# Reordering the fronts of five stages over more PSUM banks, and making the expert-choice logits inside the rotary attention

## The reference

```python
x = _layernorm(x + _L0_attn_ref(x, ...))              # latent attention, causal: 16 heads of 64, keys and values from 64 latent columns
x = _layernorm(x + _L0_xattn_ref(x, ctx_1024, ...))   # cross attention, q and k normed, rotary q: 16 heads of 16
x = _layernorm(x + _L0_ffn_ref(x, ...))               # expert choice
x = _layernorm(x + _L1_attn_ref(x, ...))              # t5 attention with a bias by relative position: 16 heads of 64
x = _layernorm(x + _L1_xattn_ref(x, ctx_1024, ...))   # cross attention, 16 heads of 16
x = _layernorm(x + _L1_ffn_ref(x, ...))               # rmsnorm, self attention, rmsnorm, mixture of experts
```

```python
logits = jnp.einsum('bsd,ed->bse', x, gate_w)
affinity = jax.nn.softmax(logits, axis=-1)
affinity = jnp.transpose(affinity, (0, 2, 1))
gating, idx = jax.lax.top_k(affinity, k)      # each expert takes its k best tokens
```

## Time and profile before

| | us |
|---|---|
| median of 3 runs | 2243.45 |
| the three runs | 2232.38, 2243.45, 2246.34 |
| the profiled execution | 2236.97 |
| its span in the trace | 2235.3 |

### The profile page before, as it was taken

How to read it: one execution, slowest core, us unless ns; L and a number is a source line. 1 busy time by engine, 2 the same in 40 slices (tenths; PEclk the granted TensorE clock), 3 DMA queues, 4 the chain that set the end, 5 groups by cost and what they waited for, 6 DMA issues and landing times. The chain is left out here.

```text
span 2235.3 us, 41856 instructions
## 1 busy us (share of the span) xinstructions
PE 1881.9 (84%) x15780; PEld 1461.0 (65%) x15780; DVE 1202.6 (54%) x2994; ACT 994.9 (45%) x2350; POOL 684.3 (31%) x609
## 2 busy tenths in 40 slices
PE   5888875899649999568999997699589996899995
PEld 4777664665539889436777775576366663788884
DVE  1666664576245545325555555366436665347774
ACT  3555552343214544326545554344234442336663
POOL 0433334673323243213323333211201001153443
PEclk9999997998569999889999999899579998899998
DMA  2000002010423352330000000100310001932334
GB/s 62 2 21 17 14 11 69 1 30 11 176 84 103 124 151 43 95 143 2 11 11 11 11 11 11 62 20 21 111 41 16 30 25 41 333 114 46 53 51 99
DMA packets 100046, 127.62 MB, mean 57 GB/s; under 512 B 8682, under 2 KB 86970, under 8 KB 99818
## 3 DMA queue, kind: packets, MB, share of 16 engines
q1 hardware_dynamic: 86554, 107.17, 14.4%
q0 software_dynamic: 13296, 17.77, 4.6%
HBM read 87.12 MB, written 39.89 MB: 57 GB/s over the span
## 5 line engine op out<-in xcount | busy, mean ns | idle before, releaser
L2049 POOL TENSOR_TENSOR L1a_probs<-L1a_probs,L1a_rinv 128x1024 f32<-128x1024 f32 x64 | 121.2, 1894 | 283.3 <-DVE L1a_rinv L2371 283.3
L2046 POOL TENSOR_TENSOR L0a_probs<-L0a_probs,L0a_rinv 128x256 f32<-128x256 f32 (+1 forms) x128 | 103.1, 826 | 205.9 <-DVE L0a_rinv L2371 205.9
L2363 DVE CUSTOM_DVE_ANT_0 L1a_sbias<-L1a_psS,L1a_bias 128x256 f32<-128x256 f32 x256 | 93.2, 421 | 123.5 <-PE L1a_psS L2180 123.5
L2294 ACT ACTIVATE L1a_probs<-L1a_sbias,L1a_nmx 128x256 f32<-128x256 f32 x256 | 126.5, 497 | 40.1 <-DVE L1a_nmx L2363 40.1
L2294 ACT ACTIVATE L0a_probs<-L0a_sbias,L0a_nmx 128x128 f32<-128x128 f32 (+1 forms) x256 | 112.8, 443 | 29.8 <-DVE L0a_nmx L2363 29.8
L3061 POOL DMA_INDIRECT moe_sums<-moe_y,moe_xg x39 | 83.8, 2149 | 134.2 <-DVE moe_y L3360 125.4
L2607 POOL DMA_INDIRECT ec_sums<-ec_yk,ec_token_at x32 | 59.0, 1844 | 192.6 <-ACT ec_yk L2760 187.8
L1589 ACT ACTIVATE L1s_pT<-L1s_psK 128x1024 f32<-128x1024 f32 x64 | 65.5, 1024 | 100.4 <-PE L1s_psK L1451 100.4
L1742 DVE TENSOR_REDUCE L1s_top<-L1s_psS 128x4 f32<-128x1024 f32 x64 | 78.3, 1226 | 58.8 <-PE L1s_psS L1436 58.8
L2832 DVE TENSOR_TENSOR ec_h<-ec_sg,ec_psU 128x512 f32<-128x512 f32 x64 | 44.0, 687 | 118.8 <-ACT ec_sg L2747 118.8
L3139 PE MATMUL moe_psY<-moe_wts,moe_hT 128*128 (+1 forms) x440 | 104.0, 379 | 0.8 <-ACT moe_hT L3206 0.8
(11 more groups left out here) (508 smaller groups left out, 4996.8 us busy)
## 6 DMA issues: line engine op xcount, KB each, us to landing
ec_wg<-in_L_ffn_w_gate SPq DMA_DIRECT2D x8, 1024.0 KB, 9.1
ec_wu<-in_L_ffn_w_up SPq DMA_DIRECT2D x8, 1024.0 KB, 13.0
ec_wd<-in_L_ffn_w_down SPq DMA_DIRECT2D x8, 1024.0 KB, 6.3
moe_rows<-blank SPq DMA_DIRECT2D x1, 5070.0 KB, 20.5
moe_xg<-moe_rows SPq DMA_DIRECT2D x39, 130.0 KB, 2.1
moe_wts<-in_L_ffn_e_gate SPq DMA_DIRECT2D x8, 512.0 KB, 9.1
moe_wts<-in_L_ffn_e_up SPq DMA_DIRECT2D x8, 512.0 KB, 9.0
moe_wts<-in_L_ffn_e_down SPq DMA_DIRECT2D x8, 512.0 KB, 9.0
```

What stands on the lines that cost most here:

```text
L2046: last = pool.tensor_tensor(v, v, bcast(rinv[:, r, :, t], 2, KEYS[t]), ALU.mult)
L2049: last = pool.tensor_tensor(v, v, bcast(rinv[:, r, :, :].rearrange("p h t -> p (h t)"), 2, S), ALU.mult)
L2294: ins = act.activation(probs[:, r, j, at], sbias[:, g % 2, j, at], ACT.Exp, bias=nmx[:, r, j, t:t + 1], scale=-1.0, accum_out=sums[:, r, j ...
L2363: last = dve.tensor_tensor_reduce(out=sbias[:, g % 2, j, at], in0=psS[:, slot + j, at], in1=added, scale=-1.0, scalar=LARGE, op0=ALU.add, ...
```

## The change

Seven edits, none of which changes what a stage computes.

1. **L0a's front.** SP issues raw_q first, and each weight has its own semaphore, so that PE starts when raw_q is there. xT moves ahead of the combined products. The items go to several banks (`FRONT_HOMES`).
2. **L0x's front.** v 0 leaves the front for the first slot of batch 0, qT and kT of batch 0 come ahead of q and k of batch 1, the filler is 6 pairs instead of 14, and DVE, POOL and SP do the same work in another order.
3. **Expert-choice logits in L0x.** `attention_stage` no longer runs the rotary stage but hands it to the expert-choice stage, which runs it with a buffer `aff` of its own. Each batch gets two more items, `turn` (four transposes of the finished batch) and `logits`; POOL raises them between its other work. The loads of `ec_x`, the turns, the logits and the powers are gone from ec.
4. **ec's loads.** SP waits for the first expert's gathered rows before it loads the second expert's weights.
5. **L1a's front.** qk 0 to 7 in a row with two heads of `turn_bias` behind each, then all of v; banks psF and psO by turns; ACT and DVE take xT before they split the weights.
6. **L1s's front.** A semaphore for each weight, xT and the weights of q and k first, items over psF, psK and psO.
7. **L1s's fill.** The zero fill of `moe_rows` goes from the front to batch 1 of SP's loop.

The core of the diff, which leaves out moved functions and what renames:

```diff
 # context_stage (L0x)
             FRONT = [(("xT",), 0), (("q", 0), 0), (("q", 1), 0), (("cT", 0), 0), (("cT", 1), 0), (("cT", 2), 0), (("k",), 0),
-                     (("v", 0), 0), (("xT",), 1), (("q", 0), 1), (("q", 1), 1), (("k",), 1),
-                     (("qT", 0), 0), (("qT", 1), 0), (("kT",), 0)]
+                     (("xT",), 1), (("qT", 0), 0), (("qT", 1), 0), (("kT",), 0), (("q", 0), 1), (("q", 1), 1), (("k",), 1)]
...
-                items = {(0, 0): [(("xT",), 2)] if b == 0 else [],
+                near = [(("kT",), b + 1), (("qT", 0), b + 1)]
+                items = {(0, 0): [(("v", 0), 0), (("xT",), 2)] if b == 0 else [],
-                         (1, 1): [(("kT",), b + 1), (("qT", 0), b + 1)],
-                         (2, 0): [(("out", 0), b - 1)],
-                         (2, 1): [(("v", b // 2 + 1), 0)] if b % 2 == 0 else [],
+                         (1, 1): near if b else [],
+                         (2, 0): [(("out", 0), b - 1)] if b else near,
+                         (2, 1): ([(("v", b // 2 + 1), 0)] if b % 2 == 0 else []) + [(("turn",), b - 2)],
-                         (3, 1): [(("xT",), b + 3)]}.get(at, [])
+                         (3, 1): [(("xT",), b + 3), (("logits",), b - 2)]}.get(at, [])
...
+        LAST = [((k,), b) for b in (B - 2, B - 1) for k in ("turn", "logits")] if rope else []
+        ORDER += LAST
...
+            def raise_logits(b):
+                wait_taken(pool, ("logits",), b)
+                pool.tensor_tensor(aff[:, :, b, :], euler[:], aff[:, :, b, :], ALU.pow).then_inc(lg_raised, 1)
...
+                if rope and st == 0 and b >= 3:
+                    raise_logits(b - 3)
...
+                elif what[0] == "turn":
+                    pe.wait_ge(x_ready, b + 1)
+                    for c in range(KD):
+                        for t in range(TT):
+                            last = pe.transpose(ps[:, c * S + t * P:c * S + (t + 1) * P], xn[:, t, c * P:(c + 1) * P], ident[:])
+                elif what[0] == "logits":
+                    wait_taken(pe, ("turn",), b)
+                    for t in range(TT):
+                        for c in range(KD):
+                            last = pe.matmul(ps[:, t * E:(t + 1) * E], xnT[:, c, t * P:(t + 1) * P], gate[:, c, :],
+                                             start=(c == 0), stop=(c == KD - 1))
...
             for what, b in FRONT:
-                item(what, b, 14 if rope and (what, b) == (("qT", 0), 0) else 0)
+                item(what, b, 6 if rope and (what, b) == (("qT", 0), 0) else 0)
 # narrow_stage (L1s)
+        FRONT_HOMES = {("qk", 1): psK[:, 0, :], ("v",): psK[:, 1, :], ("qk", 2): psO[:]}
...
-            if rms:
-                blank, rows, sums = consts[3:6]
-                sp.dma_start(rows.rearrange("(j p) d -> p j d", p=P), bcast(blank[:], 1, ROUTED)).then_inc(rows_blank, 16)
-                sp.dma_start(sums[B * S:, :], blank[:, 0:D]).then_inc(rows_blank, 16)
             for b in range(B):
...
+                if rms and b == 1:
+                    blank, rows, sums = consts[3:6]
+                    sp.dma_start(sums[B * S:, :], blank[:, 0:D]).then_inc(rows_blank, 16)
+                    sp.dma_start(rows.rearrange("(j p) d -> p j d", p=P), bcast(blank[:], 1, ROUTED)).then_inc(rows_blank, 16)
                 if rms:
                     sp.dma_start(extra_out[b, :, :, :], base[:]).then_inc(x_stored, 16)
 # wide_stage (L0a, L1a)
-            FRONT = (("xT",), ("qk", 0), ("qk", 1), ("qk", 2), ("v", 0, 0), ("v", 1, 0), ("qk", 3), ("qk", 4),
-                     ("qk", 5), ("qk", 6), ("qk", 7), ("v", 0, 1), ("v", 1, 1))
+            FRONT = (("xT",), *(("qk", p) for p in range(NP)), ("v", 0, 0), ("v", 1, 0), ("v", 0, 1), ("v", 1, 1))
...
+        FRONT_HOMES = {("q", 0): psT[:, 0, :], ("lat",): psO[:], ("q", 1): psT[:, 1, :], ("q", 3): psO[:]} if latent else \
+            {what: psO[:] for n, what in enumerate(FRONT) if n and n % 2 == 0}
...
-            load_x(0)
             if latent:
-                sp.dma_start(raw_d[:], w["Wkv_down"].rearrange("(c p) k -> p c k", p=P)).then_inc(w_in, 16)
-                sp.dma_start(raw_q[:], w["Wq"].rearrange("(c p) h k -> p c (h k)", p=P)).then_inc(w_in, 16)
+                sp.dma_start(raw_q[:], w["Wq"].rearrange("(c p) h k -> p c (h k)", p=P)).then_inc(q_in, 16)
...
+            if latent:
+                pe.wait_ge(q_in, 16)
...
+            for what in FRONT[1:] if latent else FRONT:
                 item(what, 0)
+                if what[0] == "qk":
+                    turn_bias(2 * what[1])
+                    turn_bias(2 * what[1] + 1)
 # expert_choice_stage
+        name, kind, held_in, held_out, held_w = consts[6].pop()
+        context_stage(nc, name, kind, consts, held_in, held_out, held_w, a["L0_ffn_gate_w"], aff)
...
-                for b in range(B):
-                    sp.dma_start(xt[:, b * TT:(b + 1) * TT, :], x_in[b, :, :, :]).then_inc(x_loaded[b], 16)
                 load_up(0)
...
                 load_down(0)
+                sp.wait_ge(rows_loaded[0], 16 * ST)
                 load_up(1)
                 load_down(1)
```

504 lines of the change are left out of this document (251 added, 253 removed).

## The result

| | before | after |
|---|---|---|
| median, us | 2244.32 (4 runs, 2232.38 to 2246.34) | 2170.31 (4 runs, 2169.44 to 2174.54) |
| ratio, 95% interval | | 0.9691 [0.9659, 0.9723] |
| profiled execution, its span | 2236.97, 2235.3 | 2174.54, 2172.8 |

By the ratio the change takes 3.1% off; the forecast was 2180, in a range from 2152 to 2208. By the medians it is 74 us (3.3%), by the two profiled executions 62.5: the one of before was quicker than its median by 7, the one of after slower by 4.

A forecast was written before the change was run, and what follows sets the result against it. PE was taken to bound the loops, and waits, bank turnaround and low clock the fronts. Terms -13.5 - 6 + 8 - 29.5 - 10.3 - 12 + 2.5 = -60.8 on 2236.97 give 2176.2; forecast 2180, range 2152 to 2208.

The forecast's parts named there:

- Latent front: L0a's front: PE starts at about 9.5 on raw_q, scores at 37.0 instead of 50.47: -13.5 us (-11 to -15).
- Rotary front: L0x's front: shorter filler -3.5, v 0 off the path -1.6, reordered work 1: -6 us in all (-3 to -9).
- a power still last: L0x's front: if the power of the keys is still last, the shorter filler only uncovers it: -3 us.
- Logits in the loop: Rotary loop: turns and logits add 1.57 us of PE work per batch, six batches counting: +8 us (+4 to +12).
- Seam: Expert-choice front: from last finished batch to DVE's start 8.8 us instead of 34.9: -26 us.
- Gather: Expert-choice front: with the second expert's weights held, PE's 12.84 us wait for gathered rows shortens: -3.5 us (0 to -5).
- t5 front: L1a's front: scores at 998.1 instead of 1008.46: -10.3 us (-7.5 to -13).
- Self-attention front: L1s's front: first item waits only for q and k weights, items end at 1623.2: -12 us (-7.4 at low clock).
- The fill: Self attention, batch 1: stores behind the fill land 5 us late, PE's slack takes part: +2.5 us (0 to +6).
- The slower one: Rival: turns and logits thin PE's work, rotary loop falls to 1.2 GHz; 2290 if all eight batches; chance 0.03.
- Other waits take over: Rival: fronts hang on loads, each keeping half its gain: about -25 to -35 us, 2205 to 2215; chance 0.06.
- more clock: Rival: extra work fills pauses behind which the rotary loop's clock fell: -75 us and more, about 2160 to 2165; chance 0.08.

The follow-up runs named there:

- seam_undone: Changed kernel with the expert-choice logits and powers back in their own stage, new fronts and held loads kept: 2214.97 us, ratio 0.9770.
- filler_14: Changed kernel with the 14 pairs of filler of before in the rotary front: 2177.90 us, ratio 0.9716.
- loads_unheld: Changed kernel without SP's wait for the gathered rows before the second expert's loads: 2176.69 us, ratio 0.9722.
- fronts_undone: Changed kernel with the latent, t5 and self-attention stages as before; rotary front, moved logits and held loads kept: 2242.38 us, ratio 0.9879.
- fill_at_front: Changed kernel with the 5 MB zero fill back in the self attention's front: 2189.85 us, ratio 0.9655.

## Why the prediction held, and where its terms were off

The sum was -60.8 against one execution, and 62.5 was measured. That the two lie so close is partly luck. By stages the sum missed by -1.6 (latent), -0.5 (rotary and expert choice), -4.8 (t5), +4.2 (cross, which the sum had at 0 and whose spread this is), +1.6 (self attention) and -0.8 (mixture), and within rotary and expert choice a price taken too high stands against a gain that didn't come. The steps, in its order:

- **Latent front, -13.5: -15.1** by the stage, -16.3 to the scores. Right in both halves. PE began at 8.66, not 9.5, and the scores came at 34.18, not 37.0. The other 1.9 are between the raw_o products' end and the scores, 6.8 us for a forecast of 8.7: at a clock of 1.00 the four q items followed each other without a gap, and latT's copy, which I had counted, hid behind the first of them.
- **Rotary front, -6: -5.2 to -6.9** by the y of batch 0, -6.8 by the stage (seam_undone against before). The filler's 3.5 is 3.1 by filler_14. The condition that I named (a power still last) didn't hold.
- **Logits in the loop, +8: about +4.5.** The rows' lengths were right (1.62 us for 1.57), but they aren't the price: at the full clock a batch gets 0.75 us longer, six of them 4.5. The bound of +4 was nearer. POOL's powers cost the loop nothing.
- **Seam, -26: -26.0,** with DVE's start 8.9 us after the last batch where I had 8.8; powers 20.5, the rest 5.5.
- **Gather, -3.5: -2.1 at PE, about -0.4 by the stage's end.** The step that failed. Its number for the hold was near, 3.1 by loads_unheld, but by luck: I had let PE wait for eight gathers of 1 us, where it waits for four, and one of them with its gap is 1.25; and the traffic of before wasn't the second expert's weights but the third's. Left out were two things. DVE's subtraction is now already under way when the first gather is issued; with the later issue this makes PE's wait 10.75 instead of 9.35. And behind the rows PE needed 1.7 us more to the stage's end than before, of which 1.2 are the second and third group of products, at the low clock for longer (2.76 and 1.80 instead of 1.87 and 1.52). That the whole of the wait beyond the issue is contention of DMAs, as I read the Trainium skill's rule on the shared DMA engines ("DMA: Bandwidth & Descriptors", section "Issuing engines are not separate DMA queues"), is right for the 3.1 of loads_unheld; the rest of the wait isn't traffic.
- **t5 front, -10.3: -15.5 to the scores.** The mechanism was right, three sizes were off: the strips were there 19.2 us after the stage's start, not 20.4; a qk with its two heads took some 2.70 us, not 3.0; and no 2.5 us of low clock followed, since only the first qk, in the wait for the strips, was made at it.
- **Self-attention front, -12: -12.6** in the profile, but 4.9 of it is the clock: the old front took 33.2 us to the scores in before, all five items at 1.2 GHz, and 28.3 in fronts_undone, four of them at 2.4. At like clocks the front is worth 6.6 to the scores, 9.4 by stages.
- **The fill, +2.5: +4.9,** inside its bounds of 0 to 6. I had let half of the lateness vanish in PE's slack; there is none, since y stands on the path of every batch. By the Trainium skill's "DMA: Bandwidth & Descriptors", section "Queues, rings and completion order", descriptors are consumed in ring order on each of the 16 engines; that nothing can overtake was my wording, since the section lets a later one finish its write first. The traces agree with the order: the store of base, behind the fill, landed after 18.3 us. What reached DVE is SP's 12.81 us at that issue and 7.2 for the store after it, and in fill_at_front neither is there. Put back at the front, the stage is 5 to 7 us shorter.
- **Rivals.** The slower one (the loop at 1.2 GHz) didn't come: 1.00 from 412 to 484. "Other waits take over" neither (its own terms add up to -36, not to -25 to -35); PE goes into the second expert's products without waiting for a DMA. By the medians the time lies between my forecast and "more clock", but that rival's mechanism isn't seen in the profile: the clock falls in the rotary loop as before. Why the medians differ by 74 us and the profiled executions by 62.5 no run takes apart; single executions of before spread over 14.

What stays open: why the clock of the rotary loop falls 18 us sooner in some executions of one and the same stage, which moves it by 5 to 8 us; and the gathers beside DVE's subtractions, which no run took apart.

## What to carry to other kernels

A stage's front is paid in waits and in bank turnarounds, not in work: give its items banks that the loop doesn't need yet, order its loads by first use, and put a semaphore on each. Work that only needs one batch's result belongs into the stage that makes it, on the engine that has room there; here 20 of 23 us of powers vanished in another stage's loop. What moved work costs there is the difference between two loops at the same clock, not the length of its rows. A bulk transfer that hid at a front must not be put ahead of small stores that somebody waits for: read, before moving it, when the next store behind it has to have landed.
